# Another order of VectorE's work at four places, and some matrices moved into the PSUM bank of the sums, in a fused cross-attention and mixture-of-experts layer

## The reference

```python
q = ln @ Wq.T
kv = concat([xn @ Wkv.T, ln @ Wlkv.T], axis=1)          # context keys, then own keys
qn = rmsnorm(q, qn_g) * SCALE; kn = rmsnorm(k, kn_g)
attn = softmax(where(mask, qn @ kn.T, -max)); out = attn @ v
...
x = x + tanh(g_xattn) * (out @ Wo.T + bo)
logits = layernorm(x) @ w_router; probs = softmax(logits); topk_w, topk_idx = top_k(probs, 2)
h = gelu(x_norm @ w1[e] + b1[e]); y_e = h @ w2[e] + b2[e]
x = x + tanh(g_ffn) * sum_k topk_w[k] * y_e
```

## Time and profile before

| | |
|---|---|
| time, median of 3 runs | 916.98 us (913.53 to 918.35) |
| the profiled execution's own time | 915.9 us |
| its span in the profile | 914.2 us |
| PE busy in the span | 853.0 us (93%) |
| DVE busy | 647.8 us (71%) |
| ACT busy | 514.7 us (56%) |
| POOL busy | 329.1 us (36%) |
| PE busy from 460 to 914 us (expert part) | 439.0 of 454 us |

### The profile page before, as it was taken

The page is one execution under the profiler, slowest core; times in us unless marked ns, Lnnn a source line. Parts: engine busy times, 40 slices in busy tenths (PEclk is TensorE's granted clock), DMA queues, the critical chain, the costliest instruction groups (busy, mean ns, idle before and its releaser), DMA issues.

```text
span 914.2 us, 19561 instructions
## 1 busy us (share of the span) xinstructions
PE 853.0 (93%) x5968; PEld 653.8 (72%) x5968; DVE 647.8 (71%) x1500; ACT 514.7 (56%) x1371; POOL 329.1 (36%) x241
## 2 busy tenths in 40 slices
PE   3898899998999989999999999999999999999995
PEld 3654455554455545454459999999999999999995
DVE  6767767677776767667698788876755775576694
ACT  2668676687757878558762654443533443343462
POOL 2333223423285322654144318532322322222233
PEclk9999999999999999999999999999999999999998
DMA  4801000130012201120025449452433534252282
GB/s 127 245 1 50 1 1 1 47 95 1 1 52 89 93 1 47 42 87 24 1 81 147 124 98 265 94 143 46 119 65 47 134 79 103 46 144 46 35 231 23
DMA packets 71895, 70.26 MB, mean 77 GB/s; under 512 B 18592, under 2 KB 66976, under 8 KB 71840
## 3 DMA queue, kind: packets, MB, share of 16 engines
q1 hardware_dynamic: 57696, 52.73, 19.6%
q0 software_dynamic: 13152, 16.86, 10.5%
q10 hardware_dynamic: 992, 0.00, 0.1%
HBM read 44.04 MB, written 26.31 MB: 77 GB/s over the span
## 4 chain that ended last, share of the span: by engine, by line
PE 49%; issue 16%; DVE 12%; POOL 12%; ACT 5%; DMA 4%; SPq 1%; DVEq 0%; POOLq 0%; ACTq 0%
PE psS L1689 17%; PE psF L1885 8%; PE psO L1885 8%; POOL rr L680 6%; POOL routed L690 5%; PE psO L1822 4%; PE psS L1806 3%; DVE p_sum L1140 3%; DMA lnf<-routed 2%; PE psF L1689 2%; PE psF L1853 1%; ACT sq L827 1%; ACT p_ring L871 1%; DMA xr<-in_x 1%; DVE qkd L1114 1%
## 5 line engine op out<-in xcount | busy, mean ns | idle before, releaser
L888 ACT ACTIVATE V<-psS,b_col 128x256 f32<-128x256 f32 x280 | 117.1, 471 | 208.1 <-PE psS L1689 189.6
L698 POOL DMA_INDIRECT out<-V,token_i x70 | 120.0, 1714 | 262.7 <-DVE V L1331 241.5
L680 POOL TENSOR_TENSOR rr<-ssm,minus_half 128x4 f32<-128x4 f32 (+1 forms) x72 | 119.0, 1653 | 253.8 <-DVE ssm L1104 253.7
L871 ACT ACTIVATE p_ring<-psS,shift 128x1024 f32<-128x1024 f32 x128 | 136.6, 1112 | 69.3 <-PE psS L1806 68.5
L1822 PE MATMUL psO<-p_ring,V 128*64 128x512 f32 x576 | 149.2, 615 | 0.0
L1140 DVE TENSOR_TENSOR p_sum<-p_sum,p_ring 128x1024 f32<-128x1024 f32 (+1 forms) x112 | 136.0, 1214 | 0.8
L1885 PE MATMUL psF<-ln_hi,K 128*128 128x256 f32 x560 | 123.4, 284 | 0.0
L1806 PEld LDWEIGHTS psS<-Q,K 64*128 64x128 f32 x864 | 76.1, 185 | 62.6 <-issue 43.5
L1806 PE MATMUL psS<-Q,K 64*128 64x512 f32 x864 | 120.3, 410 | 0.6 <-ACT p_ring L871 0.5
L1885 PE MATMUL psO<-ln_hi,K 128*128 128x256 f32 x560 | 120.4, 278 | 0.0
L1310 DVE TENSOR_TENSOR K<-V,K 128x512 fp32r<-128x512 f32 x140 | 97.1, 693 | 4.8
(11 more groups left out here) (289 smaller groups left out, 1758.7 us busy)
## 6 DMA issues: line engine op xcount, KB each, us to landing
xr<-in_L_ffn_w SPq DMA_DIRECT2D x11, 1024.0 KB, 4.9
xn<-in_L_ffn_w SPq DMA_DIRECT2D x11, 1024.0 KB, 6.1
lnf<-routed SPq DMA_DIRECT2D x35, 258.0 KB
routed<-pad_rows SPq DMA_DIRECT2D x17, 258.0 KB, 8.2
xr<-in_x SPq DMA_DIRECT2D x8, 512.0 KB, 4.6
xb<-in_x SPq DMA_DIRECT2D x4, 1024.0 KB, 6.2
out<-xb SPq DMA_DIRECT2D x4, 1024.0 KB, 4.7
b_raw<-in_L_ffn_b SPq DMA_DIRECT2D x11, 128.0 KB, 6.5
```

The costliest lines, as they stand in the source:

```text
L680: pool.tensor_tensor(rr[0:p, c % 2, n], ssm[0:p, c % 2, n], minus_half[0:p, n], ALU.pow).then_inc(rr_ready, 1)
L698: pool.indirect_dma_start(out_rows, bass.IndirectOffsetOnAxis(ap=token_i[:, m:m + 1], axis=0), y_out[:, m, :], None, bounds_check=NTOK - 1 ...
L871: act.activation(p_ring[0:p, u % RING, :], psS[u % 2][0:p].rearrange("p a n -> p (a n)"), ACT.Exp, bias=bias).then_inc(exp_done, 1)
L888: act.activation(g32[:, q % 2, (c % 2) * TM:(c % 2 + 1) * TM], psH[q][:, (c % 2) * TM:(c % 2 + 1) * TM], ACT.Gelu_apprx_tanh, bias=b1_col[ ...
```

## The change

VectorE's order changes at four places, and fifteen small jobs get another bank. In windows with output projections, `residual(b-1, 1)` is put ahead of `quotients` at group 1. `residual_base` leaves group 5 of the even windows: for the sequences 0 to 2 its halves are done in groups 0 and 5 of the odd window, for the last sequence in groups 5 and 8 of window 6. In windows 3 and 5 `router_logits` goes behind `mean_squares` of group 3, and `router_slots` from the start of group 7 to group 6, ahead of `scale_heads`. In `bank_uses`, output projections and norms of the groups 2, 3 and 4 take bank 7. `name[0]` is the kind of job there.

```diff
                     for name in mid_uses(w, i):
-                        yield g % 2, name
+                        yield 7 if name[0] in ("out", "norm") and 2 <= i <= 4 else g % 2, name
...
-                    if not even and past and i == (6 if last else 7):
+                    if not even and past and last and i == 6:
                         router_slots(b - 1)
                     if g >= 1:
                         add_probabilities(2 * g - 2)
-                    if not even and past and i == (2 if last else 3):
+                    if not even and past and last and i == 2:
                         router_logits(b - 1)
...
                     if tile_at(g) is not None:
                         mean_squares(tile_at(g))
+                    if not even and past and not last and i == 3:
+                        router_logits(b - 1)
                     if g >= 1 and not ahead:
                         add_probabilities(2 * g - 1)
+                    if not even and past and not last and i == 6:
+                        router_slots(b - 1)
                     if tile_at(g) is not None:
                         scale_heads(tile_at(g))
...
                         denominators(2 * w - 1)
+                    if even and past and i == 1:
+                        residual(b - 1, 1)
                     if w >= 1 and i == (1 if even else 2):
                         quotients(2 * w - 1)
...
                     if even and past:
-                        if i < 4:
+                        if i in (0, 2, 3):
                             residual(b - 1, i)
...
-                    if even and i == 5:
-                        for half in range(2):
-                            residual_base(b, half)
+                    if last and even and i in (5, 8):
+                        residual_base(b, i // 8)
+                    if more and not even and i in (0, 5):
+                        residual_base(b, i // 5)
```

## The result

The changed kernel takes 909.08 us (median of 8 runs, 907.13 to 911.83), the kernel before 917.02 us (8 runs, 913.53 to 918.47). The ratio is 0.9917 with a 95% interval of 0.9902 to 0.9933: 7.9 us or 0.8% faster. The prediction was 911.0 us. It had set 912.4 us as its bound of faster, and all eight runs of the changed kernel lie under that.

The account below looks back on a forecast made before the run. TensorE's many short waits in the attention windows were taken as the time to be won. Terms -2.0 -2.1 -3.0 +0.7 +0.6 = -5.8 us took the profiled 915.9 to 910.1, about 911.2 as a median; predicted 911 us, range 906.5 to 915.5.

Parts of the forecast that it names:

- rival (c): More is won: base hides in idle time in windows 3 and 5, bases elsewhere bring 1.5; about 908 us, chance 0.10.
- norms in bank 7, window 1: Group 3's norm loses its 2.21 us wait, then 1.4 us for scaled heads, no clock fall: -2.0 us.
- residual, windows 2, 4, 6: Put ahead of the quotients, it lets group 2's projection start 0.7 us sooner in three windows: -2.1 us.
- fourth output projection, bank 7: Output projections of groups 2 and 3 did not wait, so their new bank was to change nothing.
- bases out of windows 2, 4, 6: Out of group 5, ssm comes sooner; gain between 0.87 and 1.2, taken as 1.0 a window: -3.0 us.
- slots and base, windows 3 and 5: Base delays `ranks` about 1.0 us, slots cost 0.1 but end the wait for `base`: +0.7 us in two windows.
- logits, windows 3 and 5: `lt` about 0.6 us later at ScalarE's second norm read; group 3's norm then waits for lg: 0.3 lost, twice.
- The discount to 2.0: Window 1: 2.2 us sooner at `turn_heads` of group 4, cut to 2.0 since the heads' chain gives back a little.
- They cost and bring nothing: Bank moves of groups 2 and 4 norms, windows 3 and 5 norms, and output projections: no PE wait freed.
- not won but changes its cause: Windows 3 and 5, group 3: the norm's 1.32 us wait stays, now for lg, and 0.3 us are lost.
- The rule: Two-SBUF-input VectorE and SBUF-reading GpSimd operations exclude each other; `slot_hot` would wait for the power, 0.6 us more per window.

Follow-up runs that it names:

- the kernel with both edits: Changed kernel with logits back in their old place and the second half of the bases in group 0 of the next window: 907.16 us, second time 903.59 us.

## Why the prediction was right

The direction, the size (911.0 against 909.08, in the range) and the places were right. Its sum was -5.8 us; the attention part gave -7.95. All six terms were off the same way, towards more gain, by 0.2 to 0.5 us each, so no two errors cancelled. In number the result lies nearer to rival (c), 908 us, but what (c) rested on did not happen: the bases brought 1.12 us a window and not 1.5, and in windows 3 and 5 the base did not hide (`ranks` waits 0.91 us). Term by term:

```
                                   predicted   measured (shift)
norms in bank 7, window 1            -2.0        -2.43
residual, windows 2, 4, 6            -2.1        -2.36
fourth output projection, bank 7      0          -0.54
bases out of windows 2, 4, 6         -3.0        -3.35
slots and base, windows 3 and 5      +0.7        +0.49
logits, windows 3 and 5              +0.6        +0.25
sum                                  -5.8        -7.94
```

- **Window 1.** The step held: 1.55 us of waiting for the scaled heads where 1.4 was forecast, no fall of the clock, 3.27 us from the norm to `turn_heads` without that wait (forecast 3.3), 2.22 us at group 4 where 2.2 was worked out. The discount to 2.0 was wrong in sign: at group 5 another 0.2 us were won, with the banks alone too.
- **Residual.** The mechanism held; the size was taken from PE's own wait (0.72 us in the earlier trace rows). The gain was 0.76 to 0.81. The idle time of the weight load ahead of it fell from 1.02 to 0.23 us in window 4, by 0.79, which is the size of the gain; PE's own row did not show all of it.
- **Output projections.** "They cost and bring nothing" was wrong by 0.18 us a window, for the same reason: PE's row showed no wait, but the row of its weight loads did (0.98 us at 167.26 against 0.81 at 164.38, 0.17 less). For windows 3 and 5 the same paragraph says that the move frees PE from no wait, which the earlier trace rows contradicts: the norm of group 3 waited 1.32 us there.
- **Bases.** The bounds were 0.87 and 1.2, the value taken 1.0, measured 1.12. The forecast 0.3 us of wait is 0.38. ScalarE's squares bound it, as said.
- **Slots and base.** Both halves had the right sign and place: `ranks` waits 0.91 us (forecast 1.0), and the scaling stands 0.10 and 0.17 us behind the power, 0.07 and 0.14 more than is usual (forecast 0.1). Undone alone, the base is worth 1.1 us a window and the slots 0.9, the latter again more than PE's own wait of 0.75 us. The net is +0.24 us instead of +0.35.
- **Logits.** Here the reasoning was thin. The 0.53 us of `lt` came, but the norm of group 3 waits 0.84 us, not until the time at which it started before. The net is +0.12 us a window instead of +0.3. What the step missed is that bank 7 alone would have removed the whole 1.32 us wait: the logits' move took that back, 0.9 us a window. The prediction called this "not won but changes its cause"; the two-by-two table shows that as two cures of one wait.
- **The rule.** `slot_hot` has two SBUF inputs and ran at 242.91 in 0.28 us, while the power that began at 241.62 lasted until 243.53. VectorE was not held, as in the earlier trace rows, and the 0.6 us a window did not come. The rule (the Trainium skill, SBUF — State Buffer, Who interferes with whom) was not borne out in that direction. In the other one it may be: see below.

## What to carry to other kernels

Where two edits can each remove the same wait, count them once, and look at what each makes the other wait for: here either was worth 0.8 us a window and the pair cost 0.1. When PE is full, read the weight loads' idle time next to the matmuls': here its fall (0.79 and 0.17 us) was the gain (0.81 and 0.18), where the matmuls' own waits said 0.72 and nothing. An engine's work that has to go somewhere is cheapest where that engine waits anyway and nobody waits behind it: the same half of `residual_base` cost 1.1 us in group 5 of a window with a router and nothing in group 0 of the next.

## What the runs showed of the hardware

**The clock after a short wait.** In all four profiles in which the norm of window 1 waited 2.21 us, the granted clock fell behind it. Behind the 1.50 to 1.56 us waits for the scaled heads it did so in none of 21. In window 0 stands a wait of 1.73 to 1.76 us in every kernel; the clock fell behind it in 2 of 13 profiles and cost 1.58 us by the next group. TensorE behind that wait, in the first profile of the kernel with both edits and in its second:

```profile
74.20:77.60 3.40, 3.36 (x10) 0.53 0.01 2
```

```profile
72.80:76.20 3.40, 3.06 (x20) 1.00 0.01 2
```

In the first it is 1.2 GHz for most of the 3.4 us, in the second 2.4 GHz throughout. The kernels do the same work there, so this is chance, and it can be a part of the scatter of single runs. What in the wait decides it was not tried.

**A power beside an adding up.** A 128x4 power that starts within 0.2 us behind the start of an `add_probabilities` takes 1.91 to 1.96 us (241.62 above; 44 of them in the changed kernel). Where none runs at its start it takes 1.01: timelines of the changed kernel (group 3 of window 3, beside the logits' small operations) and of the kernel before (group 6 of window 3, VectorE idle):

```profile
222.09 1.01 POOL L680 TENSOR_TENSOR rr<-ssm,minus_half 128x4 f32<-128x4 f32 x1 [4.84 <-DVE ssm L1104]
222.68 1.22 DVE L1140 TENSOR_TENSOR p_sum<-p_sum,p_ring 128x1024 f32<-128x1024 f32 x1
```

```profile
239.11 1.01 POOL L680 TENSOR_TENSOR rr<-ssm,minus_half 128x4 f32<-128x4 f32 x1 [4.69 <-DVE ssm L1104]
```

The adding up takes 1.22 us in either case, also where it starts during the power (222.68). So it is GpSimd that seems to be held, by 0.9 us, and not VectorE in any case seen here. The ends of the powers say so too: all 45 of 128x4 that start during an adding up in the changed kernel end 0.86 to 0.91 us behind its end. One of those in each kernel starts late in the adding up and takes 1.26 us; in the kernel before it ends at 146.95, 0.87 us behind the end of the adding up of the earlier trace rows (144.86 + 1.22):

```profile
145.69 1.26 POOL L680 TENSOR_TENSOR rr<-ssm,minus_half 128x4 f32<-128x4 f32 x1
```

No kernel was built to test it; it bears on this one because the scaled heads wait some 0.9 us for the power in most groups of the attention part.
